# A two-convolution kernel with group norms: taking the differences on GpSimd, storing the last channels one by one

## What is computed

```python
x = x + _L0_conv_ref(_gn(x), L0_conv_weight, L0_conv_bias_term)      # 31 x 31, padding 15, one filter per channel
x = x + _L1_conv_ref(_gn(x), L1_conv_weight_coord, L1_conv_radius, L1_conv_weights)   # 11 x 11, padding 5
```

## Time and profile before

| | us |
|---|---|
| median of 3 runs | 3620.45 (3619.72 to 3621.17) |
| the profiled execution's own time | 3621.28 |
| its span | 3619.5 |
| PE busy | 3538.7 (98% of the span) |
| DVE busy | 3319.5 (92%) |
| ACT busy | 1191.6 (33%) |
| POOL busy | 71.3 (2%) |

### The profile page before, as it was taken

How to read it: one execution, slowest core, us unless ns; L and a number is a source line. 1 busy time by engine, 2 the same in 40 slices (tenths; PEclk the granted TensorE clock), 3 DMA queues, 4 the chain that set the end, 5 groups by cost and what they waited for, 6 DMA issues and landing times.

```text
span 3619.5 us, 60019 instructions
## 1 busy us (share of the span) xinstructions
PE 3538.7 (98%) x19008; PEld 3340.6 (92%) x19008; DVE 3319.5 (92%) x4821; ACT 1191.6 (33%) x1250; POOL 71.3 (2%) x112
## 2 busy tenths in 40 slices
PE   5899999999999999999999999999999999999996
PEld 5799999999999999999999999999999999999995
DVE  6799999999999999999999999999999999999987
ACT  3233333333333333333333333333333333333332
POOL 6100000000000000000000000000000000000000
PEclk9999999999999999999999999999999999999998
DMA  9877777788767878777878777787677777778653
GB/s 187 189 144 153 148 153 140 147 158 159 148 139 144 157 146 155 152 137 143 160 157 151 145 146 150 151 157 151 136 144 157 152 150 152 140 147 160 132 104 82
DMA packets 809998, 536.21 MB, mean 148 GB/s; under 512 B 464680, under 2 KB 772008, under 8 KB 809448
## 3 DMA queue, kind: packets, MB, share of 16 engines
q1 hardware_dynamic: 809288, 534.36, 75.4%
q10 hardware_dynamic: 544, 0.38, 0.1%
HBM read 449.06 MB, written 85.48 MB: 148 GB/s over the span
## 4 chain that ended last, share of the span: by engine, by line
PE 94%; SPq 1%; DVE 1%; DMA 0%; issue 0%; ACT 0%; POOL 0%; DVEq 0%; POOLq 0%
PE acc L1037 94%; SPq L435 1%; DMA toep<-padded 0%; DVE xt L842 0%; DVE y_image L869 0%; DVE yt L859 0%; SPq L445 0%; DVE xt L835 0%; POOL raw L587 0%; POOL raw L590 0%; ACT raw L679 0%; DVE x_lo L849 0%; ACT x_hi L642 0%; DVE raw L877 0%; ACT images L634 0%
## 5 line engine op out<-in xcount | busy, mean ns | idle before, releaser
L1037 PE MATMUL acc<-x_hi,toep 128*112 128x448 f32 (+3 forms) x12672 | 3381.9, 348 | 70.2 <-DVE x_lo L849 40.1
L1037 PEld LDWEIGHTS acc<-x_hi,toep 128*112 128x112 f32 x12672 | 2261.2, 181 | 203.7 <-issue 54.6
L1037 PE MATMUL acc<-x_lo,toep 128*112 128x448 f32 (+3 forms) x6336 | 2209.3, 349 | 0.0
L1037 PEld LDWEIGHTS acc<-x_lo,toep 128*112 128x112 f32 x6336 | 1142.4, 180 | 64.2
L642 ACT ACTIVATE x_hi<-xt 128x1440 fp32r<-128x1440 f32 x384 | 541.2, 1409 | 1778.9 <-DVE xt L842 1778.9
L849 DVE TENSOR_TENSOR x_lo<-xt,x_hi 128x1440 fp32r<-128x1440 f32 x384 | 629.5, 1639 | 76.6 <-ACT x_hi L642 75.5
L859 DVE TENSOR_TENSOR yt<-acc,p 128x896 f32<-128x896 f32 x384 | 415.9, 1083 | 105.6 <-PE acc L1037 104.7
L634 ACT ACTIVATE images<-raw,norm 128x896 f32 (+1 forms) x384 | 440.0, 1146 | 50.1 <-DVE norm L819 50.1
L842 DVE TENSOR_TENSOR xt<-xt 128x960 f32<-128x960 f32 x384 | 445.4, 1160 | 7.9
L826 DVE BATCH_NORM_STATS2 part<-raw 96x6 f32 (+3 forms) x768 | 449.2, 614 | 1.3
L835 DVE STREAM_TRANSPOSE xt<-images 128x960 f32<-128x960 f32 x384 | 444.9, 1159 | 2.8 <-ACT images L634 1.3
(11 more groups left out here) (54 smaller groups left out, 230.5 us busy)
## 6 DMA issues: line engine op xcount, KB each, us to landing
toep<-padded SPq DMA_DIRECT2D x384, 276.0 KB
toep<-padded SPq DMA_DIRECT2D x384, 234.0 KB
toep<-padded SPq DMA_DIRECT2D x384, 186.0 KB
out_dram<-raw SPq DMA_DIRECT2D x192, 336.0 KB, 5.0
raw<-in_x_dram SPq DMA_DIRECT2D x93, 672.0 KB, 10.4
toep<-padded SPq DMA_DIRECT2D x768, 58.5 KB
toep<-padded SPq DMA_DIRECT2D x384, 69.0 KB
toep<-padded SPq DMA_DIRECT2D x384, 47.2 KB
```

The lines of the kernel that those rows point to most:

```text
L1037: last = nc.tensor.matmul(dst, toeplitz(toep, f, place, part, k), src[:, h, cols], start=(m == matrices[0][0] and part == 0 and src is x_h ...
```

## The change

- From iteration 2 on, `differences` run on POOL instead of DVE, for the jobs of iterations 2 to 33. The jobs of iterations 0 and 1 keep them on DVE.
- The differences of both kinds of job are written to one shared place of `xt` (`AT_D`), with the transposed even columns on one side of it and the odd ones on the other, so that each kind of operand is still one stretch.
- For those jobs `low` moves behind `transpose_out` in a FIRST slot, and behind `add_residual` in a SECOND slot.
- On ACT, from iteration 2 on, `copy_p2` goes ahead of `high` in FIRST slots too, and `root` ahead of `high` in all.
- `images` has one place instead of two.
- At the very end, the last three channels are stored one at a time, each behind its own wait, instead of together behind the last one.

```diff
--- before.py
+++ after.py
@@ -58,9 +58,10 @@
 JE = JH + 1
 N_D = JE * B
 N_OP = 3 * N_D
-AT_ODD = 2 * JE
-AT_EVEN = AT_ODD + JE
-N_T = AT_EVEN + (JE + 1) + 2 * JE
+AT_EVEN = 0
+AT_D = JE + 1
+AT_ODD = AT_D + 2 * JE
+N_T = AT_ODD + JE
 CP = 96
 CT = C // CP
 K1, K2 = 31, 11
@@ -71,7 +72,7 @@
 H_RING = 3
 P_RING = 2
 T_RING = 2
-I_RING = 2
+I_RING = 1
 AHEAD = 2
 FIRST, SECOND = 1, 2
 
@@ -183,6 +184,11 @@
 MEASURED_SECOND_GROUP = {6: [0, 1, 2], 8: [3, 4, 5]}
 NORM1_SLOT = 8
 LAST_FIRST = FIRST_SLOTS[-1]
+
+
+def on_gpsimd(i):
+
+    return not isinstance(i, int) or i >= 2
 
 
 def norm2_group(i, s):
@@ -384,13 +390,12 @@
         def repeated_odd():
             return xt_view(AT_ODD, [[0, 2], [1, N_D]])
 
-        def differences_of(s):
-            start = 0 if PATTERN[s][0] == FIRST else AT_EVEN + 1 + JE
-            return xt_view(start, [[N_D, 2], [1, N_D]])
+        def differences_held():
+            return xt_view(AT_D, [[N_D, 2], [1, N_D]])
 
         def operand(s):
 
-            start = 0 if PATTERN[s][0] == FIRST else AT_EVEN + 1
+            start = AT_D if PATTERN[s][0] == FIRST else AT_EVEN + 1
             return xt[:, start * B:start * B + N_OP]
 
         def raw_rows(g, c):
@@ -527,9 +532,10 @@
                 iteration(i)
             for k in range(GROUPS - 2, GROUPS + 2):
                 iteration(k)
-            sp.wait_ge(residual_added, SLOTS * GROUPS)
-            store(GROUPS - 1, CG // 2, CG)
-            sp.wait_ge(out_stored, 16 * BANDS * 2 * GROUPS)
+            for c in range(CG // 2, CG):
+                sp.wait_ge(residual_added, SLOTS * GROUPS - (CG - 1 - c))
+                store(GROUPS - 1, c, c + 1)
+            sp.wait_ge(out_stored, 16 * BANDS * (2 * GROUPS + CG // 2 - 1))
 
 
         @block.gpsimd
@@ -619,6 +625,23 @@
             clear(2, area1_zeroed)
             filters_low(2)
 
+            def differences(i, s):
+
+                n = job(i, s)
+                pool.wait_ge(xt_ready, n + 1)
+                sequences = (shifted_even(), repeated_odd())
+                nc.gpsimd.tensor_tensor(differences_held(), *(sequences if PATTERN[s][0] == FIRST else sequences[::-1]),
+                                        ALU.subtract).then_inc(xd_ready, 1)
+
+            def iteration(i):
+                for s in slots(i):
+                    differences(i, s)
+
+            with pool.Fori(2, GROUPS) as i:
+                iteration(i)
+            iteration(GROUPS)
+            iteration(GROUPS + 1)
+
 
         @block.scalar
         def _(act):
@@ -629,8 +652,8 @@
                 norm = norm1 if conv == FIRST else norm2
                 if c == 0:
                     act.wait_ge(norm_chain, (norm_ordinal(conv, g) + 1) * NORM_STEPS)
-                if positive(n - 1):
-                    act.wait_ge(xt_ready, n - 1)
+                if positive(n + 1 - I_RING):
+                    act.wait_ge(xt_ready, n + 1 - I_RING)
                 nc.scalar.activation(image(ring(i, s, I_RING))[:, :, 1:1 + W], raw_rows(g, c), ACT.Identity,
                                      bias=norm[:, 0:1], scale=norm[:, 1:2]).then_inc(xn_ready, 1)
 
@@ -737,15 +760,18 @@
                 for s in slots(i):
                     after, then = later(i, s, AHEAD), later(i, s, AHEAD + 1)
                     group2 = norm2_group(i, s)
-                    if PATTERN[s][0] == SECOND:
+                    copy_first = PATTERN[s][0] == SECOND or on_gpsimd(i)
+                    if copy_first:
                         copy_p2(i, s)
-                    if after:
+                    if after and not on_gpsimd(i):
                         high(*after)
                     if s == NORM1_SLOT and not (peeled and (i == 0 or i >= GROUPS - 1)):
                         root(i * 2 + 1)
                     if group2 is not None:
                         root(norm2_ordinal(group2))
-                    if PATTERN[s][0] == FIRST:
+                    if after and on_gpsimd(i):
+                        high(*after)
+                    if not copy_first:
                         copy_p2(i, s)
                     if peeled and i == 0 and job(i, s) == CG - 1 - AHEAD:
                         root(1)
@@ -839,7 +865,7 @@
                 n = job(i, s)
                 dve.wait_ge(xt_ready, n + 1)
                 sequences = (shifted_even(), repeated_odd())
-                nc.vector.tensor_tensor(differences_of(s), *(sequences if PATTERN[s][0] == FIRST else sequences[::-1]),
+                nc.vector.tensor_tensor(differences_held(), *(sequences if PATTERN[s][0] == FIRST else sequences[::-1]),
                                         ALU.subtract).then_inc(xd_ready, 1)
 
             def low(i, s):
@@ -960,7 +986,7 @@
                     if after:
                         transpose_in(*after)
                     if conv == FIRST:
-                        if after:
+                        if after and not on_gpsimd(after[0]):
                             differences(*after)
                         if measure_before:
                             statistics2(*before)
@@ -973,15 +999,18 @@
                             statistics(part1, parts1_ready, i + 1, c1)
                         if s == NORM1_SLOT and measure_next:
                             normalisation(i * 2 + 1, i + 1, part1, parts1_ready, norm1, job(i, LAST_FIRST) + 1)
-                        if after:
+                        low_first = after and not on_gpsimd(after[0])
+                        if low_first:
                             low(*after)
                         outputs(i, s)
                         transpose_out(i, s)
+                        if after and not low_first:
+                            low(*after)
                         add_residual(i, s)
                     else:
                         if measure_before:
                             statistics2(*before, (0,))
-                        if after:
+                        if after and not on_gpsimd(after[0]):
                             differences(*after)
                         if group2 is not None:
                             statistics2(*before, (1,))
```

## The result

| | before | changed |
|---|---|---|
| runs beside each other, median us | 3620.09 (3619.42 to 3621.17, 4 runs) | 3656.48 (3655.89 to 3657.56, 4 runs) |
| ratio to before | | 1.0099, 95% interval 1.0087 to 1.0112 |
| profiled execution: time, span | 3621.28, 3619.5 | 3656.55, 3654.5 |

The account below looks back on a forecast made before the run. PE was taken to bound the steady part, so only the end could win: 3621.28 - 1.6 (queue) - 2.3 (last store) = 3617.4, or 3616.5 us against the runs, counted as the same; range 3612.5 to 3628.

Parts of the forecast that it names:

- POOL's differences: Each job's differences on POOL, from iteration 2 on, were to take 2.3 us and cost PE nothing.
- The layout of the ordinary slots: DVE's new order over a pair of jobs: `low` ends 3.8 us after the FIRST job's end, PE wants it at 5.3.
- rival 1(c): SECOND slots: POOL also holds `outputs`, 1.7 us each, 2.4 late, 3644 us; chance 0.19 together with the rival's other forms.
- the last store: At the span's end, storing a third of the data takes 4.8 us instead of 7.1, a gain of 2.3 us.
- the queue: SP's loads and stores in the tail: J5 starts 1.0 us earlier and runs 0.6 shorter, a gain of 1.6 us.
- That delays the chain by 0.4 us: 0.7 late of 1.5: Slot 2: POOL holds the norm chain only from its first two-input step; `outputs` 0.7 us late, within the margin.
- rival 1(b): Slot 2: POOL holds the chain's first copy, 1.8 us, 2.1 late, 0.6 by 30, 3635 us; 0.19 with the other forms.
- The lateness without a hold: Slot 2, without POOL's delay: `outputs` due at 18.7 us instead of 18.4, 0.3 late.
- The margin: After a FIRST job's end `low` ends at 3.8 us and PE wants it at 5.3: 1.5 us to spare.
- `copy_p2` ahead of `high` costs nothing: FIRST slots on ACT: `copy_p2` waits until about 9.7 us, and `high` is not due before 15.2.
- J2 starts: In the tail, with `low` moved and the last norm chain later, J2 starts 1.5 us later, at 3551.2.
- The gap before J5: In the tail, PE's idle time between J4's end and J5's start falls from 6.3 us to 3.7.

Follow-up runs that it names:

- experiment 8: The changed kernel with `agg` in spare columns of the PSUM image and the other pair's statistics in slot 10 instead of slot 2; 3617.25 us.
- experiment 7: The kernel before, with an unused one-input POOL instruction of 96 x 960 added in slots 2 and 8 of iterations 2 to 31; 3620.51 us.
- Experiment 6: The kernel before, with an unused two-input POOL instruction of 96 x 960 added in slots 2 and 8 of iterations 2 to 31; 3638.99 us.
- experiment 1: The changed kernel with `agg`, which the norm chain's first copies read, in spare columns of PSUM instead of SBUF; 3622.98 us.
- experiment 9: Experiment 8 plus tail differences on DVE, ACT's order by the prepared job's iteration, J2's `low` directly behind `outputs`, two stores behind the tail's loads; 3608.08 us.
- experiment 5: The kernel before with only its last three channels stored one at a time; 3616.95 us.

## Why the prediction was wrong

**What held.** PE was the bound, and DVE's relief by itself returned nothing (experiment 8). POOL's differences took 2.26 us (2.3 forecast). The layout of the ordinary slots was right to 0.15 us: `low` ended at 3.85 to 3.95 (3.8). `outputs`, the ordinary case of rival 1(c), isn't held. Of the end, 4.8 us came against 3.9. That the sum is near is partly luck, for its two terms missed in opposite directions: the last store gave 3.6 (2.3 forecast), the queue 1.2 (1.6).

**The step that failed** is "That delays the chain by 0.4 us: 0.7 late of 1.5". It let the chain run beside POOL up to its first two-input step, L797. The chain stopped at its first copy, half a us in, which is the mechanism of rival 1(b), and the delay is 1.76 us. The evidence that I set against it was weak. Rows 4 show four copies in 0.83 us beside a POOL instruction with **one** input and 121 elements; experiment 7 shows that with one input, DVE gets in between. And in that very row the first copy was held a little, 260 ns instead of 159, which the sum of four hid:

```profile
23.60 0.26 DVE L788 COPY halves<-agg 32x4 f32<-32x4 f32 x1
```

Experiment 6 shows it with two inputs: held to the end. I had the rule in hand and let a row that did not meet its case overrule it. The Trainium skill (SBUF — State Buffer, Who interferes with whom) says that the lock is exclusive and that copies in a two-port mode take it. Beside a two-input POOL instruction this case agrees (1923 ns instead of 160 in SBUF, at most 165 from PSUM). Beside a one-input one, a copy took 573 ns and was over 1.6 us before POOL: a lock held for the whole instruction isn't what is seen.

**Three smaller terms of the same sum**, all on the side that favoured the change:
- The lateness without a hold was put at 0.3 us. It is 2.37 - 1.76 = 0.61 (in experiment 1: 1.28 - 0.57 = 0.71). The start had been laid out by steps over a whole pair of jobs, and some 0.3 us got lost in them.
- The margin was put at 1.5 us, up to 5.3. `low` ending at 4.92 costs nothing, and at 5.07 it costs 0.18 a time, so the margin is 1.1 to 1.25 us. I had taken the load in SP's queue for the end of the job. PE starts the next job 0.2 us before the mark, at 5.11, and in experiment 1 `low` at 5.07 already made its first weight load late.
- From `low` to PE at work there is a step that the sum didn't have: `low` ends at 6.14, the first matmul starts at 6.27 (0.13), and the second follows 0.30 behind it, not 0.20.

With the measured terms rival 1(b) would have read 0.61 + 1.76 = 2.37 late; `low` ends at 2.37 + 3.77 = 6.14; (6.14 + 0.13 + 0.30 - 5.31) x 30 = 37.8 us, against the 18 that it stood at. It was one share of 0.19: the mechanism was named, and priced at half.

**"`copy_p2` ahead of `high` costs nothing"** passed over the one slot where the new order isn't in place yet. In iteration 1's last FIRST slot ACT still runs `high` first, and this is the first `high` that waits for POOL. So `copy_p2` came late, `outputs` with it, and PE waited. The timeline there (DVE, then PE):

```profile
233.07 1.09 DVE L885 TENSOR_TENSOR yt<-acc,p 128x896 f32<-128x896 f32 x1 [4.32 <-ACT p L675]
...
237.10 0.46 PE L1069 MATMUL acc<-x_hi,toep 128*112 128x448 f32 x1 [0.81 <-DVE x_lo L875]
```

It costs 1.1 us, and experiment 9 takes it away. The order was chosen by the iteration of the slot, where the wait belongs to the job that is prepared.

**The end**, by its terms: J2 starts 17.27 us behind the last FIRST job's end instead of 15.32, 1.95 later (1.5 forecast), because the last norm chain is held too: its first copy, at 3581.80, took 618 ns instead of 159, and those 0.46 us are the difference. The gap before J5 is 4.55 us (3.7). The middle value for the last store was the wrong choice: it took 3.5 us (4.8 forecast; 2.4 by its data alone), and experiment 5 gives the same.

The 0.9 us ahead of iteration 2 belong to the execution, not to the change: the mark at 231.0 us in it lies between 229.7 and 230.6 in the profiles of the kernel before and of all nine experiments, four of which have the changed kernel's start. What stays open is which property of the POOL instruction decides between a hold to the end and one that lets DVE in between. From experiment 6 to 7 the number of inputs changed, but with it the operation (a subtraction, then a product with a constant) and the length (1.78, then 2.60 us).

## To carry to other kernels

An operation moved to GpSimd isn't free for VectorE because it is off its list: ask which VectorE instructions will stand beside it, and count small float32 copies and tensor-scalar steps in SBUF as held until a two-input GpSimd instruction ends (steps of one element per partition ran freely here). Where a serial chain of small steps is on the path, put its input in PSUM, which took 1.1 us off the lateness here; to start it behind GpSimd's end is a second way, not tried. And lateness costs nothing until the margin is used up, then nearly its full length in every iteration: here two reliefs of 1.1 us in the one critical slot each returned some 33 us of 36, and both together only 6 more.

## What was not expected of the hardware

- A copy of 32 x 4 float32, 160 ns long, is held for up to 1923 ns beside a two-input GpSimd instruction (128 x 960, 2263 ns) when it reads SBUF, and never in 256 times when it reads PSUM. A VectorE `tensor_scalar` of 32 x 7 is held too (780 ns instead of 218); one of 32 x 1 is not (141 to 143 ns). The chain's small two-input steps weren't met by it in the main loop, and `outputs` with one operand in PSUM wasn't held.
- Beside a one-input GpSimd instruction of the same size (2602 ns), the same copy loses 0.41 us and is over 1.6 us before GpSimd; a later `tensor_scalar` of 32 x 7 is then held until GpSimd ends (650 to 669 ns).
- PE loses time without showing idle: with `low` done 0.04 us before the next job's usual start, only a weight load shows a gap of 0.30 us, and the pair of jobs takes 18.54 us instead of 18.36.
